# Splitting four of eight Toeplitz blocks of a long convolution into three products, in place of two

## What is computed

```
x = x + einsum('bct,bcd->bdt', x, W0[condition])      # 64x64 matrix per batch
x = x + down(silu(gate(x)) * up(x))                   # 1024 -> 2752 -> 1024, with LoRA parts per batch
x = x + mask * (causal convolution of x with K + D*x) # one filter K[h, 0:1024] per channel h
x = x + einsum('bct,bcd->bdt', x, W3[subject]) + b3   # 64x64 matrix per batch
```

## Time and profile before

| | before |
|---|---|
| median of three runs | 1816.24 us |
| the profiled execution: its time | 1816.11 us |
| its span, first to last instruction | 1814.5 us |
| mean granted TensorE clock | 0.978 |
| TensorE busy over the span | 95%, 8904 matmuls |
| VectorE, ScalarE, GpSimd busy | 62%, 38%, 10% |
| convolution stage, first matmul to last | 1625.2 to 1771.8 us |
| DMA traffic | 269.52 MB, mean 149 GB/s |

### The profile page before, as it was taken

How to read it: one execution, slowest core, us unless ns; L and a number is a source line. 1 busy time by engine, 2 the same in 40 slices (tenths; PEclk the granted TensorE clock), 3 DMA queues, 4 the chain that set the end, 5 groups by cost and what they waited for, 6 DMA issues and landing times.

```text
span 1814.5 us, 29058 instructions
## 1 busy us (share of the span) xinstructions
PE 1715.8 (95%) x8904; PEld 1470.7 (81%) x8904; DVE 1129.6 (62%) x1695; ACT 687.0 (38%) x1095; POOL 175.2 (10%) x282
## 2 busy tenths in 40 slices
PE   5679999999998999998999999999989899999998
PEld 5568888888888888886888888888877778879997
DVE  2566676676665554334666766766657843448887
ACT  3233333333333443232333333333323422236655
POOL 3442000000000000000000000000010004402330
PEclk9789999999999999999999999999989999999999
DMA  5787233233325564554333333332325534467754
GB/s 196 216 272 212 94 112 102 92 107 103 99 87 197 174 214 162 206 175 147 111 102 99 103 105 98 107 104 90 101 80 182 177 133 140 162 240 238 240 178 186
DMA packets 106660, 269.52 MB, mean 149 GB/s; under 512 B 17142, under 2 KB 22038, under 8 KB 105590
## 3 DMA queue, kind: packets, MB, share of 16 engines
q1 hardware_dynamic: 81334, 210.54, 35.6%
q0 software_dynamic: 12544, 36.29, 6.2%
q10 hardware_dynamic: 12736, 22.16, 3.2%
HBM read 225.12 MB, written 61.64 MB: 158 GB/s over the span
## 4 chain that ended last, share of the span: by engine, by line
PE 44%; DVE 5%; issue 1%; SPq 1%; ACT 1%; DMA 0%; ACTq 0%; DVEq 0%
PE ps L1070 30%; PE ps L1320 5%; PE ps L1317 3%; PE ps L1108 2%; PE ps L1349 1%; DVE whl L1721 1%; PE ps L1333 1%; SPq L435 1%; PE ps L1145 1%; PE ps L1147 1%; DVE act_hl L1725 0%; DVE x1s L1735 0%; SPq L432 0%; DMA wraw<-in_wd 0%; ACT whl L744 0%
## 5 line engine op out<-in xcount | busy, mean ns | idle before, releaser
L1070 PE MATMUL ps<-act_hl,whl 128*128 128x512 f32 x2016 | 466.0, 393 | 10.6 <-DVE act_hl L1725 7.1
L1070 PE MATMUL ps<-xop,aop_a 128*128 128x512 f32 x2016 | 474.4, 391 | 0.0
L1070 PEld LDWEIGHTS ps<-act_hl,whl 128*128 128x128 f32 x2016 | 379.8, 189 | 95.1 <-DVE act_hl L1725 11.5
L1070 PEld LDWEIGHTS ps<-xop,aop_a 128*128 128x128 f32 x2016 | 374.1, 189 | 74.5
L1070 PE MATMUL ps<-xop,aop_b 128*128 128x512 f32 x1512 | 367.7, 392 | 6.8 <-DVE t L1687 6.7
L1070 PEld LDWEIGHTS ps<-xop,aop_b 128*128 128x128 f32 x1512 | 280.1, 189 | 61.9 <-DVE t L1687 6.9
L1721 DVE TENSOR_TENSOR whl<-wraw,whl 128x1024 fp32r<-128x1024 f32 x96 | 118.9, 1238 | 244.7 <-ACT whl L744 244.2
L744 ACT ACTIVATE whl<-wraw 128x1024 fp32r<-128x1024 f32 (+2 forms) x132 | 114.9, 887 | 357.9 <-PE ps L1070 289.1
L1658 DVE TENSOR_TENSOR aop_b<-raw,aop_b 128x512 fp32r<-128x512 f32 x84 | 58.0, 691 | 107.7 <-ACT aop_b L744 107.6
L744 ACT ACTIVATE aop_a<-asum 128x512 fp32r<-128x512 f32 x84 | 48.7, 625 | 163.9 <-DVE asum L1650 160.2
L1108 PEld LDWEIGHTS ps<-t_hl,lb_hl 128*128 128x128 f32 x672 | 97.2, 190 | 9.9
(11 more groups left out here) (222 smaller groups left out, 2020.3 us busy)
## 6 DMA issues: line engine op xcount, KB each, us to landing
wraw<-in_wd SPq DMA_DIRECT2D x88, 512.0 KB, 3.4
raw<-in_wgu SPq DMA_DIRECT2D x168, 256.0 KB, 3.1
rtoep<-k_dram SPq DMA_DIRECT2D x64, 512.0 KB, 4.6
lb_raw<-bgu_of_batches SPq DMA_DIRECT2D x84, 256.0 KB, 3.9
act_raw<-act_dram SPq DMA_DIRECT2D x84, 256.0 KB, 3.4
act_dram<-t ACTq DMA_DIRECT2D x42, 256.0 KB, 2.0
act_dram<-u ACTq DMA_DIRECT2D x42, 256.0 KB, 2.0
xn<-in_x SPq DMA_DIRECT2D x16, 512.0 KB, 6.5
```

The source lines that it names most:

```text
L1070: ins = pe.matmul(bank, wt, r, start=start and k == 0 and n == 0, stop=stop and k == nk - 1 and n == 2, skip_group_check=True)
```

## The change

`SPLIT` goes from 2 to 4: blocks 2 and 3 of each channel, with 192 and 160 columns, become three products of split operands instead of plain fp32. `TS` goes from 256 to 512 with it, so `toep_h` and `toep_l` have 512 columns, and the copy into `toep` takes 512 columns instead of 768. A channel has 12 split matmuls and 8 plain ones in the trace. The larger tiles take the room in which `w3hi` and `w3lo` lay; these two get new addresses behind `ostage`.

```diff
-SPLIT = 2
+SPLIT = 4
 TS = SPLIT * P
...
         (u_hl, toep_h, toep_l), at = place(xr_base, [
             ("u_hl", [P, URING, 2, KB * B], F32R), ("toep_h", [P, TRING, TS], F32R),
             ("toep_l", [P, TRING, TS], F32R)])
-        assert at <= xr_base + KB * TOK * 4
-        (w3hi, w3lo), at = place(xr_base + KB * TOK * 4, [
-            ("w3hi", [P, PAIRS, P], F32R), ("w3lo", [P, PAIRS, P], F32R)])
         assert at <= top
-        (yv, x2hi, x2lo, ostage), _ = place(top, [
+        (yv, x2hi, x2lo, ostage, w3hi, w3lo), _ = place(top, [
             ("yv", [P, 2, KB, B], F32), ("x2hi", [P, 2, T], F32R), ("x2lo", [P, 2, T], F32R),
-            ("ostage", [P, 2, T], F32)])
+            ("ostage", [P, 2, T], F32), ("w3hi", [P, PAIRS, P], F32R), ("w3lo", [P, PAIRS, P], F32R)])
```

## The result

The changed kernel took 1825.81 us, the median of six executions (1823.82 to 1832.61), against 1816.76 for the kernel before in the same rounds: 9.05 us more. The means of the two stand at a ratio of 1.0055 with a 95% interval of 1.0033 to 1.0078. The median is 0.3 us above the range given, and the rise is nearly twice the 5.15 us forecast. A second series, run with the experiments, gave 1829.59 (1.0068, 1.0048 to 1.0087).

A forecast was written before the change was run, and what follows sets the result against it. TensorE was taken to bound the stage, VectorE a near second. Longer channels 4.4, slow first channels 0.2, stage end 0.45 and slow last channel 0.1 sum to +5.15 us: 1821.3 us, range 1817.3 to 1825.5.

The forecast's parts named there:

- The new step of 0.112 us, +0.076 a channel: TensorE, blocks 2 and 3: eight split steps replace six in 0.82 us, +4.4 us over 58 channels.
- The count of 58 channels: Convolution stage: channels on TensorE without one wait, 126.44 / 2.18, each charged 0.076 us.
- ScalarE, nothing: Copies into `toep_h` and `toep`: one gains what the other loses, about 625 ns each, no cost.
- VectorE hides, with 0.1 us to spare: Steady channel: `toep_l` takes 0.28 us more, but VectorE's work stays under TensorE's 2.256 us.
- The floor of 2.15 us: VectorE's own work per channel after the change: 1.87 us start-to-start plus 0.28, its instructions overlapping.
- The price if the cover goes: Rival, chance 0.12: VectorE bounds the channel at 2.29 us; 1823.2 us in all, 1829 with signal latency.
- The first channel's start doesn't move: Start of the convolution: the longer `toep_l` fits before the input's high part, no cost.
- The end of the stage, +0.45: Stall ahead of the last channel: VectorE's last `toep_l` meets GpSimd's `w3lo`, +0.45 us, bounds 0 and +0.7.
- the first of the two outcomes: End of the stage: `toep_l` comes before `w3lo` and holds GpSimd 0.28 us longer.
- The half-clock channels, +0.1, +0.1, +0.1: First, second and last channels at reduced clock: dearer steps cost +0.1 us in each.
- no rival of mine: Rivals: VectorE as bound, 0.12; steps follow columns, stage no longer, 0.09; low step of 0.105 to 0.108, 0.11.

The follow-up runs named there:

- e7: Changed kernel plus 19 unread TensorE products ahead of the stage, blocks 2 and 3 without their low-part product: 1834.18 us, ratio 1.0098 to before.
- e9: Changed kernel plus 19 unread TensorE products ahead of the stage, fourth layer's weights split in 16 pieces inside the convolution loop: 1830.98 us, ratio 1.0080 to before.
- e5: Changed kernel plus 19 unread TensorE products in the wait ahead of the stage, to keep the clock: 1820.95 us, ratio 1.0019 to before.
- e6: Kernel before plus 19 unread TensorE products in the wait ahead of the stage: 1816.13 us, ratio 0.9995 to before.
- e4: Changed kernel with `SPLIT = 3`, so only the 192-column block is newly split: 1818.17 us, ratio 1.0005 to before.
- e1: Kernel before, run again unchanged: 1816.89 us, ratio 0.9996 to before.
- e2: Changed kernel with `SPLIT` back at 2, so only the addresses of `w3hi` and `w3lo` moved: 1818.31 us, ratio 1.0005 to before.

## Why the prediction was right in kind and short in size

- **The new step of 0.112 us, +0.076 a channel: right.** Measured 2.253 instead of 2.256. Splitting replaces two matmuls that their columns limit by three that their weight loads limit. By the 107 ns for a load that the Trainium skill gives ("TensorE: Matmul & The Clock Gate", section "LDWEIGHTS (loading the stationary operand)") it would have been +0.036; the measured +0.073 decides for 0.112. The count of 58 channels was one short: the 59th, up to 1761.19, is still on the chain ahead of the stall, worth 0.07 us.
- **ScalarE, nothing: right**, 633 + 617 ns for what was 420 + 830.
- **VectorE hides, with 0.1 us to spare: right, more narrowly.** It idles 0.04 us a channel. The floor of 2.15 us was right too (2.13 in e7's first channels). The price if the cover goes was put at 2.29 us, or 2.39 with signals; it is 2.41 in e7 and 2.51 in e9, but by another mechanism than instructions that don't overlap: the copy of GpSimd landing on `x1s` or `toep_l`.
- **"The first channel's start doesn't move": wrong by 0.3 us.** I let `toep_l` fit before the input's high part at its free-running length; it is held up by GpSimd's copies there and becomes the path.
- **The end of the stage, +0.45: about right**, +0.35, by the first of the two outcomes.
- **The half-clock channels, +0.1, +0.1, +0.1: this is the step that failed.** I took the stretch as long as the one trace had it and priced only the steps within. The term is what the stretch costs in all. It isn't a constant: 6.3 us in one execution of the changed kernel, 12.8 in another, against 3.2 to 6.0 at `SPLIT = 2`. Each channel more at half clock is +2.0 us. With the clock held, the change costs 4.8 us (e5 against e6), without it 9 to 12; so the 4 to 7 us missing from the forecast are this term, which the sum had at 0.3, and no rival of mine had it.
- The 9 us of the first measurement were not seen in the profile pair: its 8.4 us hold 4.6 of scatter ahead of the stage, which by luck stood in for the slow channels that other executions had.

What stays open is why the clock stays at half for longer with twelve split and eight plain matmuls than with six and twelve, though TensorE shows busy all along. The wait ahead of the stage, 0.3 us longer in the changed kernel, is an unlikely cause: e4 has a shorter one (4.14 us, against 4.52 before) and 9.8 us at half clock. The runs show that the clock stays down longer, by the mean clocks above all, since a few traces at each `SPLIT` overlap (6.0 and 6.3 us), and what removing it is worth; they don't show the cause.

## What to carry to other kernels

Before trading one kind of matmul for another, follow single weight loads, not mean durations: from 192 columns down, the two plain fp32 matmuls of a block beat the three split ones here, since each matmul takes a load of 0.112 us at least, and at 224 columns the split ones win. Where TensorE idles ahead of a dense stage, price the half-clock stretch by more than one execution, and fill the wait. And an engine at 93% of the period is a bound in waiting: which of its instructions falls together with a neighbour's depends on who waits for whom, and the one that does can grow by more than the slack. In e7 `x1s` grew by 0.37 us; the changed kernel had 0.04 to spare.

## What the runs showed that I had not expected

A kernel with two weight loads a channel fewer (e7, 18 instead of 20) ran 13 us slower than e5. And the stage began at 1625.2, 1628.2 and 1630.3 us in three executions with `SPLIT` at 2 (before, e1, e2) whose spans lie within 2.5 us: a single pair of traces doesn't place a difference of 5 us.
